# A tower block of attention and mixture of experts: one half of each weighing goes between the next group's two units of scores, the other half behind that group's fill

## The chip, the cores and the metric

One NeuronCore of one Trainium2 chip runs the whole program. The metric is the device time of one execution in microseconds (us), here the median of three runs.

## The reference

The input is x, 4 images of 64 channels and 64 x 64 pixels. Three steps follow one another:

```python
h = tok(x)                    # 1x1 conv, batch norm, relu, 1x1 conv to 9 filters per pixel,
                              # then each pixel is the sum of its 3x3 neighbours times those filters
h = h + attn(layernorm(h))    # 4 images, 4096 rows of 64: softmax(Q K^T / 8) V, one head
h = h + ffn(layernorm(h))     # each row of 64 goes to the best of 32 experts: 64 -> 16 -> 64, relu
```

In attention Q, K and V are the layer norm's rows times a 64 x 64 matrix plus a bias; each of the 4096 rows of an image is weighed against all 4096 rows of it. All is fp32.

## The kernel before, in words

**Blocks and groups.** An image is four blocks of 1024 query rows, so there are 16 blocks n. Each block's attention runs over 16 groups g of 256 key rows. Q K^T is folded into one matrix: `g_t` holds a block's queries times that matrix, `keys_t` the transposed layer norm's rows. A group has two units of scores (`score`, L573), each four matmuls of 64x64 by 64x512 into half of the PSUM tensor `scores`. In the profile an fp32 matmul is two records, so such a unit is eight. Behind each unit ScalarE takes the exponential of 128x1024 scores into a slot of `probs` (L736), a ring of four slots. Weighing (`into_z`, L583) multiplies a group's exponentials with `keys` and adds into `z_ps`, over all 16 groups of a block: eight matmuls, four for each of two tiles r of keys. The two exponentials of a group are both needed for either tile.

**The order on TensorE** is written out by hand, in the loop over n and g at the end of the TensorE program (from L658). In each group stand: the two units of scores of group g, then the fills of the group, then the weighing of group g-1. The weighing of a block's last group, 15, comes in the next block's group 0, behind its two units of scores. VectorE then waits for `pv_done`, adds the two halves of `z_ps` into `z_sb` (L1011, L1013) and raises `z_copied`; the first weighing of the new block waits for that.

**Fills** are the other work of TensorE. A table (`opening_groups` to `whole_plan`, from L79) says which fills stand in which group. Those the text speaks of, for a block m whose attention is done (behind(m), groups of the next block): `pz` in group 3 (z times the value matrix, L521; VectorE drains it from L918 on, and goes on to the residual and the second layer norm), `yt` in 6 (transposes, L448), `lg` in 7 (router logits, L527; drained by VectorE at L928), `fin` in 8 (transposes of block m-1's expert output, L564; it waits until lg is drained, as both use the same PSUM banks), `ot` in 10, `hid0` to `hid3` in 11 to 14 (first expert matrix, L539 and L543; ScalarE drains them at L729) and `o2` in 15 (L556). For blocks to come: `cc` and `cv` (the two small convolutions, L483 and L493; cc or cv stands in group 1 of blocks 1, 2, 4, 6, 8 and 10), `xt` (L448) and `g` (L513), which turn the layer norm's rows into `keys_t` and `g_t`. In block 0, xt stands in groups 3, 7 and 11, g in 4, 8 and 12, and the scores of groups 4, 8 and 12 wait for ScalarE's copy of xt (L721).

**VectorE** works its list in order: z's copy, then `sum0`, `sum1`, `sum2` (the taps of the dynamic convolution of a block four ahead, L856 and L861, in groups 0, 2 and 4 of the plan, then its layer norm), with pz between sum1 and sum2 and lg behind sum2. Blocks 12 to 15 have no sums. In block 0 it works the sums of blocks 1 to 3, whose filters come by DMA.

Of the kernel before, what the change touches and what calls it, by code (L numbers as in the profile page):

```python
# [24 lines left out]
BLOCKS = B * NQ  # L25
PAIRS = TILES // 2
# [133 lines left out]
def vit_block_kernel(nc, x, once, kept, out):  # L160
# [5 lines left out]
    with ExitStack() as ctx:  # L166
# [3 lines left out]
        def sem(name):  # L170
            return ctx.enter_context(nc.semaphore(name))
# [76 lines left out]
        scores_ready, probs_ready, pv_done = sem("scores_ready"), sem("probs_ready"), sem("pv_done")  # L248
        scores_ready_again, probs_ready_again = sem("scores_ready_again"), sem("probs_ready_again")
        pv_done_again = sem("pv_done_again")  # L250
        z_copied = sem("z_copied")
# [14 lines left out]
        def groups_of(n):  # L266

            return [(g, plan[n].get(g, [])) for g in range(-1, PAIRS + 1)]
# [13 lines left out]
        def rows_of(r):  # L282
            return slice(64 * r, 64 * r + 64)
# [136 lines left out]
        def _(pe):  # L420
# [6 lines left out]
            def wait_drained(fill):  # L427
                pe.wait_ge(drained[banks_of.sem[fill]], banks_of.nth[fill])
# [140 lines left out]
            def score(n, g, c):  # L569

                for r in range(2):
                    for h in range(2):
                        last = T.matmul(scores[rows_of(h), c, r * 512:(r + 1) * 512],  # L573
                                        keys_t[rows_of(r), n // NQ % 2, g * 128 + 64 * h:g * 128 + 64 * h + 64],
                                        g_t[rows_of(r), n % GRING, c, :], start=True, stop=True)
                return last

            def into_z(n, g):

                for r in range(2):  # L580
                    for h in range(2):
                        for c in range(2):
                            last = T.matmul(z_ps[rows_of(c), h, :], keys[rows_of(h), n // NQ % 2, 2 * g + r, :],  # L583
                                            probs[rows_of(h), (2 * g + c) % RING, r * 512:(r + 1) * 512],
                                            start=(g == 0 and r == 0), stop=(g == PAIRS - 1 and r == 1))
                return last

            def usual_score(n, g):
                for c in range(2):
                    unit = (n * PAIRS + g) * 2 + c  # L590
                    if unit > 1:
                        pe.wait_ge(probs_ready, unit - 1)
                    score(n, g, c).then_inc(scores_ready, 1)

            def usual_weigh(n, g):
                if g == 0 and n:
                    pe.wait_ge(z_copied, n)
                pe.wait_ge(probs_ready, (n * PAIRS + g) * 2 + 2)
                into_z(n, g).then_inc(pv_done, 1)

            def attend_again():
                into_z(0, PAIRS - 1)
                for g in range(PAIRS):
                    for c in range(2):
                        if g or c:
                            pe.wait_ge(probs_ready_again, max(1, 2 * g + c - 1))
                        score(0, g, c).then_inc(scores_ready_again, 1)
                    if g:
                        pe.wait_ge(probs_ready_again, 2 * g)
                        into_z(0, g - 1).then_inc(pv_done_again, 1)  # L610
                pe.wait_ge(probs_ready_again, 2 * PAIRS)
# [35 lines left out]
            def shift_if_needed(b):  # L647
                pe.wait_ge(flag_ready, 1)
                with pe.If(pe.value_load(flag[0:1, 0:1], min_val=0, max_val=1)):
                    find_max(b)  # L650
                    if b == 0:
                        attend_again()
                with pe.Else():
                    pe.sem_inc(max_scores_ready, 4 * TILES)
                    pe.sem_inc(shifted_ready, S // 512)

            pe.wait_ge(kept_first_loaded, 16)
            for n in range(BLOCKS + 1):  # L658
                b = n // NQ
                if n % NQ == 0 and 0 < b < B:  # L660
                    wait_drained(f"xt@{n + NQ - 1}")
                    wait_drained(f"g@{n + NQ - 1}")
                    shift_if_needed(b)
                for g, names in groups_of(n):
                    if n < BLOCKS and 0 <= g < PAIRS:
                        if n == 0 and g % (PAIRS // NQ) == 0:
                            wait_drained(f"xt@{g // (PAIRS // NQ)}")
                        if g == 0:
                            wait_drained(f"g@{n}")
                        if n == 0 and g == 0:  # L670

                            pe.wait_ge(flag_ready, 1)
                        usual_score(n, g)
                    if g == 0 and n:
                        usual_weigh(n - 1, PAIRS - 1)
                    for full in names:
                        fill(full)
                    if n < BLOCKS and 0 < g < PAIRS:
                        usual_weigh(n, g - 1)
                if n == 0:  # L680
                    shift_if_needed(0)
                    pe.wait_ge(pool_weights_ready, 1)
# [411 lines left out]
```

## Time and profile before

| | us |
|---|---|
| median of 3 runs | 1241.97 (1240.64 to 1242.17) |
| the profiled execution | 1238.29 |
| its span, first to last instruction | 1236.2 |
| TensorE matmul busy | 1156.3 |
| ScalarE busy | 623.8 |
| VectorE busy | 496.5 |
| mean granted TensorE clock | 0.984 |

The profile is one execution, and the rows further down are all from it. Rows of matmuls give the start of the first record, and the time to the modelled end of the last one. Matmuls on different quarters of the array run at the same time.

### The profile page before, as it was taken

The page shows a single profiled execution, that of the slowest core. Times are in us where ns is not written, and L with a number is a line of the kernel's source. Part 1 is how long each engine was busy: PE and PEld are TensorE (multiplying, and loading weights), DVE is VectorE, ACT ScalarE, POOL GpSimd, SP SyncE. Part 2 cuts the span into 40 slices and gives each one's busy share as a digit, 9 for nine tenths or more (in the row PEclk, how much of TensorE's full clock was granted, in tenths as well). Part 3 has the DMA queues.
Part 4 walks back from the last instruction along what each step waited for, and adds up shares of the span by engine and source line. Part 5 has one row for each costly group of instructions (what it writes and reads, how often), then busy time and mean ns, then how long its engine had stood idle before and what let it go on. Part 6 is the DMA issues. An engine that isn't in the chain of part 4 may idle for free.

```text
span 1236.2 us, 28064 instructions
## 1 busy us (share of the span) xinstructions
PE 1156.3 (94%) x12122; PEld 464.9 (38%) x12122; DVE 496.5 (40%) x1130; ACT 623.8 (50%) x664; POOL 10.1 (1%) x36
## 2 busy tenths in 40 slices
PE   7698999999999999999999999999999999999965
PEld 2133434333343433434343333434334333434431
DVE  4882774518072452707245170724403030313131
ACT  1255555555555455555555555554555555554611
POOL 3000000000000000000000000000000000000000
PEclk9999999999999999999999999999999999999986
DMA  5543231201214120121212012121000000000000
GB/s 139 120 114 89 70 89 27 63 2 31 57 28 98 27 61 1 32 58 28 60 28 55 10 34 54 27 62 27 10 2 10 1 2 10 1 10 1 10 1 18
DMA packets 11886, 48.42 MB, mean 39 GB/s; under 512 B 2462, under 2 KB 2590, under 8 KB 11372
## 3 DMA queue, kind: packets, MB, share of 16 engines
q1 hardware_dynamic: 11756, 46.53, 15.8%
q8 instruction: 101, 1.65, 0.6%
q14 instruction: 29, 0.24, 0.1%
HBM read 41.77 MB, written 4.75 MB: 38 GB/s over the span
## 4 chain that ended last, share of the span: by engine, by line
PE 68%; DVE 20%; DVEq 4%; issue 4%; ACT 2%; DMA 2%; SPq 0%; ACTq 0%
PE z_ps L583 26%; PE scores L573 24%; PE both L556 5%; DVEq L803 4%; PE both L543 4%; DVE hres L861 4%; DVE tap_product L856 2%; PE both L448 1%; PE z_ps L473 1%; DVE tap_product L828 1%; DVE tap_product L826 1%; DVE stat L824 1%; DVE stat L830 1%; DMA filter_ring<-filters 1%; ACT hidden L729 1%
## 5 line engine op out<-in xcount | busy, mean ns | idle before, releaser
L736 ACT ACTIVATE probs<-scores 128x1024 f32<-128x1024 f32 x480 | 465.4, 1021 | 472.7 <-PE scores L573 472.7
L573 PE MATMUL scores<-g_t,keys_t 64*64 64x512 f32 x4096 | 506.1, 592 | 3.1 <-issue 2.9
L583 PE MATMUL z_ps<-probs,keys 64*64 64x512 f32 x4096 | 506.6, 593 | 0.2 <-DVE z_sb L1013 0.2
L573 PEld LDWEIGHTS scores<-g_t,keys_t 64*64 64x64 f32 x4096 | 170.3, 134 | 281.8 <-issue 275.7
L583 PEld LDWEIGHTS z_ps<-probs,keys 64*64 64x64 f32 x4096 | 160.7, 133 | 230.3 <-issue 204.6
L946 DVE COPY o_sb<-both 128x512 f32<-128x512 f32 x16 | 11.1, 692 | 487.0 <-PE both L556 487.0
L861 DVE TENSOR_TENSOR hres<-hres,tap_product 128x504 f32<-128x504 f32 (+1 forms) x128 | 88.0, 688 | 10.8 <-issue 0.5
L856 DVE SCALAR_TENSOR_TENSOR tap_product<-filter_ring,w,xin 128x504 f32<-128x504 f32 (+1 forms) x120 | 89.0, 742 | 6.1 <-DMA filter_ring<-filters 2.2
L729 ACT ACTIVATE hidden<-both 128x1024 f32<-128x1024 f32 x64 | 65.5, 1023 | 10.0 <-PE both L543 10.0
L543 PE MATMUL both<-y_t,w 64*64 64x512 f32 x512 | 70.0, 618 | 0.0
L556 PE MATMUL both<-hidden,w 64*64 64x512 f32 x512 | 66.2, 604 | 0.0
L736 ACT ACTIVATE probs<-scores,first_scale 128x1024 f32<-128x1024 f32 x32 | 34.1, 1111 | 22.7 <-PE scores L573 22.5
L1011 DVE COPY z_sb<-z_ps 128x512 f32<-128x512 f32 x16 | 11.1, 692 | 81.9 <-PE z_ps L583 81.9
L556 PEld LDWEIGHTS both<-hidden,w 64*64 64x64 f32 x512 | 27.1, 136 | 25.0 <-issue 23.6
L513 PE MATMUL both<-keys_t,a_w 64*64 64x512 f32 x128 | 18.2, 639 | 14.7 <-ACT hidden L729 12.6
L539 PE MATMUL both<-onehot_t,mask_w 64*64 64x512 bf16 x256 | 26.3, 392 | 4.2 <-ACT hidden L729 3.4
L543 PEld LDWEIGHTS both<-y_t,w 64*64 64x64 f32 x512 | 20.2, 138 | 22.7 <-issue 18.9
L564 PE MATMUL both<-w,o_sb 64*64 64x64 f32 x512 | 11.3, 228 | 15.3 <-DVE logits L928 13.6
L725 ACT COPY g_t<-both 128x1024 f32<-128x1024 f32 x16 | 16.2, 1012 | 16.7 <-PE both L513 16.7
L448 PE MATMUL both<-w,keys 64*64 64x64 f32 x512 | 10.9, 225 | 13.8 <-DVE keys L837 13.8
L828 DVE TENSOR_TENSOR tap_product<-tap_product 128x512 f32<-128x512 f32 x32 | 22.2, 693 | 2.4
L830 DVE TENSOR_REDUCE stat<-tap_product 128x8 f32<-128x512 f32 x32 | 22.0, 686 | 2.3
(113 smaller groups left out, 542.9 us busy)
## 6 DMA issues: line engine op xcount, KB each, us to landing
filter_ring<-filters SPq DMA_DIRECT2D x90, 384.0 KB, 5.4
out_dram<-out_sb SPq DMA_DIRECT2D x32, 128.0 KB, 2.4
xin<-x_dram SPq DMA_DIRECT2D x6, 528.0 KB, 7.4
hidden<-once_dram SPq DMA_DIRECT2D x1, 930.0 KB, 12.8
hidden<-once_dram SPq DMA_DIRECT2D x1, 576.0 KB, 4.5
filters<-filters_sb SPq DMA_DIRECT2D x30, 18.0 KB
xin<-x_dram SPq DMA_DIRECT2D x1, 384.0 KB, 6.2
xin<-x_dram SPq DMA_DIRECT2D x1, 368.0 KB, 7.3
```

The source lines that it names most:

```text
L539: T.matmul(both[rows_of(c), r, :], mask_w[rows_of(r), f * 128 + 64 * c:f * 128 + 64 * c + 64], onehot_t[rows_of(r), :], start=True, stop=F ...
L543: last = T.matmul(both[rows_of(c), r, :], w1[rows_of(r), f * 128 + 64 * c:f * 128 + 64 * c + 64], y_t[rows_of(r), :], start=False, stop=True)
L556: last = T.matmul(both[rows_of(r), h, :], w2[rows_of(h), f, :], hidden[rows_of(h), f, r, :], start=(f == 0 and h != r), stop=(f == FT - 1))
L573: last = T.matmul(scores[rows_of(h), c, r * 512:(r + 1) * 512], keys_t[rows_of(r), n // NQ % 2, g * 128 + 64 * h:g * 128 + 64 * h + 64], g ...
L583: last = T.matmul(z_ps[rows_of(c), h, :], keys[rows_of(h), n // NQ % 2, 2 * g + r, :], probs[rows_of(h), (2 * g + c) % RING, r * 512:(r + ...
L729: A.activation(hidden[:, int(name[3:]), :, :], both[:, :, :], ACT.Relu).then_inc(done, 1)
L736: A.activation(probs[:, unit % RING, :], scores[:, c, :], ACT.Exp, scale=SCALE if n else first_scale[:, 0:1]).then_inc(probs_ready, 1)
L803: dve.drain()
L828: V.tensor_tensor(squares[:, :, :], centred[:, :, :], centred[:, :, :], ALU.mult)
L830: V.reduce_sum(total, squares[:, :, :], AX_X)
L856: product = V.scalar_tensor_tensor(dst, flt, keep["b2c"][:, t:t + 1], pix, ALU.add, ALU.mult)
L861: V.tensor_tensor(mine[:, :, lo:hi], mine[:, :, lo:hi], dst, ALU.add)
```

## The change

`into_z` takes the tiles of keys that it is to weigh. `usual_score` is one unit, `usual_weigh` one tile r of the two; the first tile has the waits (for `z_copied` in group 0, and for both exponentials), the second raises `pv_done`. In a group the order is now: scores unit 0, weighing of the group before with tile 0, scores unit 1, fills, weighing of the group before with tile 1. The other engines' programs are not touched.

```diff
-            def into_z(n, g):
-
-                for r in range(2):
+            def into_z(n, g, tiles=range(2)):
+
+                for r in tiles:
...
-            def usual_score(n, g):
-                for c in range(2):
-                    unit = (n * PAIRS + g) * 2 + c
-                    if unit > 1:
-                        pe.wait_ge(probs_ready, unit - 1)
-                    score(n, g, c).then_inc(scores_ready, 1)
-
-            def usual_weigh(n, g):
-                if g == 0 and n:
-                    pe.wait_ge(z_copied, n)
-                pe.wait_ge(probs_ready, (n * PAIRS + g) * 2 + 2)
-                into_z(n, g).then_inc(pv_done, 1)
+            def usual_score(n, g, c):
+                unit = (n * PAIRS + g) * 2 + c
+                if unit > 1:
+                    pe.wait_ge(probs_ready, unit - 1)
+                score(n, g, c).then_inc(scores_ready, 1)
+
+            def usual_weigh(n, g, r):
+                if r == 0:
+                    if g == 0 and n:
+                        pe.wait_ge(z_copied, n)
+                    pe.wait_ge(probs_ready, (n * PAIRS + g) * 2 + 2)
+                last = into_z(n, g, [r])
+                if r:
+                    last.then_inc(pv_done, 1)
+
+            def behind_by_one(n, g):
+                return (n, g - 1) if g else (n - 1, PAIRS - 1)
...
-                        usual_score(n, g)
-                    if g == 0 and n:
-                        usual_weigh(n - 1, PAIRS - 1)
+
+                        for k in range(2):
+                            usual_score(n, g, k)
+                            if k == 0 and (n or g):
+                                usual_weigh(*behind_by_one(n, g), 0)
+                    elif g == 0:
+                        usual_weigh(*behind_by_one(n, g), 0)
                     for full in names:
                         fill(full)
-                    if n < BLOCKS and 0 < g < PAIRS:
-                        usual_weigh(n, g - 1)
+                    if 0 <= g < PAIRS and (n or g) and (n < BLOCKS or g == 0):
+                        usual_weigh(*behind_by_one(n, g), 1)
```

On TensorE, at the change from block 2 to block 3 (rows in pairs: the first matmul of a unit with its waits, then the others of it). Before, from the last weighing of block 2 to the first of block 3:

```order
L583 MATMUL z_ps<-probs,keys 64x512 [waits probs_ready]
L583 MATMUL z_ps<-probs,keys 64x512 x7
L573 MATMUL scores<-g_t,keys_t 64x512 [waits probs_ready]
L573 MATMUL scores<-g_t,keys_t 64x512 x3
L573 MATMUL scores<-g_t,keys_t 64x512 [waits probs_ready]
L573 MATMUL scores<-g_t,keys_t 64x512 x3
L583 MATMUL z_ps<-probs,keys 64x512 [waits probs_ready,z_copied]
L583 MATMUL z_ps<-probs,keys 64x512 x7
```

Now, from the second half of the last weighing of block 2 to the first unit behind the wait:

```order
L583 MATMUL z_ps<-probs,keys 64x512 x4
L573 MATMUL scores<-g_t,keys_t 64x512 [waits probs_ready]
L573 MATMUL scores<-g_t,keys_t 64x512 x3
L583 MATMUL z_ps<-probs,keys 64x512 [waits probs_ready,z_copied]
L583 MATMUL z_ps<-probs,keys 64x512 x3
L573 MATMUL scores<-g_t,keys_t 64x512 [waits probs_ready]
```

The second unit of scores has moved from before the wait for `z_copied` to behind it.

On TensorE around fin (L564, 16 transposes) in group 8 of block 3, between lg (L527) and the weighing behind fin. Before:

```order
L527 MATMUL both<-router_w,y_t 128x64 x4
L583 MATMUL z_ps<-probs,keys 64x512 x8
L573 MATMUL scores<-g_t,keys_t 64x512 x8
L564 MATMUL both<-w,o_sb 64x64 x16
L583 MATMUL z_ps<-probs,keys 64x512 x8
```

Now:

```order
L527 MATMUL both<-router_w,y_t 128x64 x4
L583 MATMUL z_ps<-probs,keys 64x512 x4
L573 MATMUL scores<-g_t,keys_t 64x512 x4
L583 MATMUL z_ps<-probs,keys 64x512 x4
L573 MATMUL scores<-g_t,keys_t 64x512 x4
L564 MATMUL both<-w,o_sb 64x64 x16
L583 MATMUL z_ps<-probs,keys 64x512 x4
```

Between the two fills stand four units as before, but half of group 7's weighing now stands ahead of fin, where all of it stood behind.

## Rows read from the trace of the kernel before

**Rows 1.** The page: busy time of TensorE, and the chain that ended last by engine

```profile
PE 1156.3 (94%) x12122; PEld 464.9 (38%) x12122; DVE 496.5 (40%) x1130; ACT 623.8 (50%) x664; POOL 10.1 (1%) x36
...
PE 68%; DVE 20%; DVEq 4%; issue 4%; ACT 2%; DMA 2%; SPq 0%; ACTq 0%
```

**Rows 2.** The page's groups: busy us, mean ns of one, idle before

```profile
L736 ACT ACTIVATE probs<-scores 128x1024 f32<-128x1024 f32 x480 | 465.4, 1021 | 472.7 <-PE scores L573 472.7
```

**Rows 3.** Timeline, middle of block 3: start us, us, engine, what

```profile
276.63 1.90 PE L573 MATMUL scores<-g_t,keys_t 64*64 64x512 f32 x16
...
277.74 1.94 ACT L736 ACTIVATE probs<-scores 128x1024 f32<-128x1024 f32 x2 [1.59 <-PE scores L573]
...
278.35 1.90 PE L583 MATMUL z_ps<-probs,keys 64*64 64x512 f32 x16
```

**Rows 4.** Timeline, change from block 2 to block 3

```profile
271.02 2.27 PE L583 MATMUL z_ps<-probs,keys 64*64 64x512 f32 x16
...
272.73 2.27 PE L573 MATMUL scores<-g_t,keys_t 64*64 64x512 f32 x16
...
273.36 0.69 DVE L1011 COPY z_sb<-z_ps 128x512 f32<-128x512 f32 x1 [3.70 <-PE z_ps L583]
...
274.12 0.69 DVE L1013 TENSOR_TENSOR z_sb<-z_sb,z_ps 128x512 f32<-128x512 f32 x1
...
274.87 1.95 PE L583 MATMUL z_ps<-probs,keys 64*64 64x512 f32 x16
```

**Rows 5.** Timeline, change from block 3 to block 4, with a fill (L483)

```profile
345.89 0.69 DVE L1013 TENSOR_TENSOR z_sb<-z_sb,z_ps 128x512 f32<-128x512 f32 x1
...
346.22 1.41 PE L483 MATMUL both<-xin,conv_w 64*64 64x512 f32 x8
...
347.08 2.27 PE L583 MATMUL z_ps<-probs,keys 64*64 64x512 f32 x16
```

**Rows 6.** Timeline, pz and what VectorE starts behind it, blocks 3, 4, 5

```profile
281.89 1.16 PE L521 MATMUL both<-wv_w,z_sb 128*128 128x130 f32 x8
...
283.11 0.17 DVE L918 RECIPROCAL stat<-both 128x4 f32<-128x4 f32 x1
...
354.43 1.16 PE L521 MATMUL both<-wv_w,z_sb 128*128 128x130 f32 x8
...
355.63 0.18 DVE L918 RECIPROCAL stat<-both 128x4 f32<-128x4 f32 x1 [0.66 <-PE both L521]
...
425.84 1.16 PE L521 MATMUL both<-wv_w,z_sb 128*128 128x130 f32 x8
...
427.42 0.18 DVE L918 RECIPROCAL stat<-both 128x4 f32<-128x4 f32 x1
```

**Rows 7.** Timeline, lg drained by VectorE, and fin, block 3

```profile
303.38 0.42 DVE L928 COPY logits<-both 128x256 f32<-128x256 f32 x1
...
303.85 0.69 PE L564 MATMUL both<-w,o_sb 64*64 64x64 f32 x32 [1.81 <-DVE logits L928]
```

**Rows 8.** Waits: engine, line, for whom: us in total, times, longest

```profile
DVE stat L918 <- PE both L521: 38.4, 11, 8.3
...
PE both L564 <- DVE logits L928: 13.6, 11, 1.8
...
PEld z_ps L583 <- DVE z_sb L1013: 7.1, 9, 1.1
```

**Rows 9.** Timeline, the last xt of block 0

```profile
102.79 0.69 PE L448 MATMUL both<-w,keys 64*64 64x64 f32 x32 [3.03 <-DVE keys L837]
...
103.28 1.93 PE L583 MATMUL z_ps<-probs,keys 64*64 64x512 f32 x16
...
103.54 0.59 ACT L721 COPY keys_t<-both 128x512 f32<-128x512 f32 x1 [2.46 <-PE both L448]
```

**Rows 10.** Stretches: us, busy by engine, granted clock (1.00 is full), DMA, GB/s

```profile
269.00:341.00 72.00, 69.05 (x754) 27.41 (x750) 30.86 (x70) 37.54 (x40) 0.00 (x0) 1.00 0.16 38
...
84.00:87.00 3.00, 3.00 (x16) 0.96 (x12) 2.76 (x5) 0.12 (x1) 0.00 (x0) 0.50 0.00 0
```

## The prediction

> **What bounds the kernel now.** I read the page's head and groups first, then the timeline at the places where the order changes, and the waits last. TensorE is busy 1156.3 us, 94% of the span, and carries 68% of the chain that ended last; VectorE carries 20% [rows 1]. ScalarE is no bound: an exponential takes 1021 ns of it for every two units of TensorE [rows 2]. I call four fp32 matmuls of 64x512 a unit (eight records), whether they are one unit of scores or half a weighing. In the middle of a block, pieces of two units start 1.72 us apart (276.63, 278.35), so a unit costs 0.86 us [rows 3]. There nothing is waited for, and regrouping the same units can win nothing by itself. What the change can move is what TensorE waits for at the few places where another engine answers:
> - *z at the change of block.* The last weighing of block 2 ends at 271.02 + 2.27 = 273.29; VectorE adds the two halves until 274.81, and the first weighing of block 3 starts at 274.87, 1.58 after that end [rows 4]. Two units of scores stand between and hide nearly all of it: the ends 273.29 and 276.82 are 3.53 apart where four units need 3.43, so 0.10 is lost. (I compare ends, since matmuls can start in pairs, skewed, with no gain in rate.) Where a fill stands there too, as in block 4, nothing is lost: the ends 347.63 and 349.35 are 1.72 apart [rows 5].
> - *pz in group 3.* Its result goes to VectorE, which is there just then: in block 3 it starts 0.06 after the fill's end (281.89 + 1.16 = 283.05, start 283.11), in block 4 it has waited 0.66, in block 5 it comes 0.42 late [rows 6].
> - *fin in group 8* waits until VectorE has drained lg: 1.81 us in block 3 [rows 7], 13.6 us over 11 times [rows 8]. VectorE is on the path from z through pz to here.
> - *xt in block 0*, which waits for VectorE's layer norm: 3.03 us at the last of them [rows 9].
>
> **The change, part by part.** No instruction's work is added or taken away; 4 matmuls of each weighing move to before the second unit of scores of the next group.
>
> (a) *The wait for z.* The last half of block n-1 now ends after both of block n's first two units of scores, and one unit, not two, stands before the next block's first half, which waits for z. VectorE's part is the same 1.58 us. From the end E of the last half: scores end at E + 0.86, the half starts at E + 1.58 and ends 1.09 later (the row of two units after such a wait is 1.95 long [rows 4], less 0.86) at E + 2.67, where E + 1.72 would be due: 0.95 lost. Behind the wait stand the second unit of scores, then the fill of group 1, which gives no cover any more. Extra at each change of block: 0.95 - 0.10 = 0.85 without a fill there, 0.95 with one. Blocks 1, 2, 4, 6, 8 and 10 have the fill.
>
> (b) *What VectorE then waits for.* From z's release to pz there were 8 units (7.02 us with the restart, 274.87 to 281.89 [rows 4, 6]); now 10, as the halves of scores 1 and weighing 2 shift across. So in block 3 pz ends at 274.87 + 7.02 + 1.72 + 1.16 = 284.77 and VectorE goes on at 284.81 by the 0.04 of block 4: 1.70 later than before. Its run to lg, and with it fin, comes 1.70 later; TensorE arrives at fin 1.72 later, so the wait of 1.81 there stays. The steps between (yt in group 6 behind y, xt behind the layer norm) move with both. In block 4 z is released at 345.89 + 0.69 + 0.06 = 346.64; 10 units and the fill's one give pz at 346.64 + 7.02 + 1.72 + 0.86 = 356.24 for 354.43: 1.81 later, and VectorE the same, since it had been waiting already. In block 5: pz ends at 427.00 + 1.72, VectorE goes on at 428.76 for 427.42: 1.34.
>
> (c) *One unit less behind the fills.* Since a half now goes ahead of each fill, one unit less is left between fin and the next z: -0.86 in each block. Net per block: with a fill 1.81 - 0.86 = 0.95 (six blocks: 5.7); blocks 3, 9, 11 as block 3, 1.70 - 0.86 = 0.84 (2.5); blocks 5, 7 as block 5, 1.34 - 0.86 = 0.48 (1.0). I sort them by the 11 waits at L918 [rows 8]: six of about 0.66 and five of the light blocks leave five blocks that come late. Blocks 12 to 15 have neither fin on the path nor sums: 4 x 0.85 = 3.4.
>
> (d) *Block 0.* Its last xt is set by VectorE and DMA, which the change does not touch, and one unit less is left behind it: -0.86. But the next scores need ScalarE's copy of xt (103.54 + 0.59 = 104.13) and now have one unit of cover, 103.28 + 0.86 = 104.14 [rows 9]: about 0.06 back. Net -0.8.
>
> (e) *The half's wait for exponentials.* It needs the second exponential of the group before. That unit of scores ends at e; by the timeline the exponential starts 0.07 later (the first unit ends at 276.63 + 1.90 - 0.86 = 277.67, the exponential starts at 277.74 [rows 3]), takes 1.02, and 0.06 later the half may start: e + 1.15. It is due at e - 0.18 + 1.72 = e + 1.54. In skewed stretches (rows of 2.27 instead of 1.90) the start is due at e - 0.57 + 1.72 = e + 1.15: no margin, no loss. ScalarE's drains of fills still fit, as a group is as long as before. Costed at nothing; the cover is 0.39 us, and if it went, each group would pay the rest.
>
> (f) *More changes between scores and weighings*, some 500 of them more. [Rows 3] show such a change in step with the rest; to the 0.01 the rows resolve, it could be worth 5 us either way, and I take zero, as the starts there stand 1.72 apart like any two pieces.
>
> Sum: 5.7 + 2.5 + 1.0 + 3.4 - 0.8 = **+11.8 us**. The profiled execution took 1238.29 (span 1236.2) and would take 1250.1; the median of the three runs is 1241.97, 3.7 above it, so I forecast 1253.8.
>
> **A rule that speaks against it more.** The granted clock stood at full, 2.4 GHz, through block 3 with its wait of 1.81 (1.00), and stood at half of it, 1.2 GHz, at 84 to 87 us, behind the opening [rows 10]. The Trainium skill, "TensorE: Matmul & The Clock Gate", section "A second HAM failure mode: psum-queue depth-cycling", says that brief pauses between groups of matmuls can make the clock swing between its levels; by it the sum would have a term of its own for the clock instead of none (its size by rows: case 3 below). The trace disagrees so far: waits at fin as long as the new one, in block after block, did not do it.
>
> **The rivals.**
> 1. *Not slower: fin swallows the delay.* If VectorE were not held at pz, the wait at fin would shrink by up to 1.81 us. The ten blocks 2 to 11 would pay 5 x 0.95 + 5 x 0.85 = 9.0 and get back nearly all of the 13.6 us [rows 8], say 13.3; block 1 and blocks 12 to 15 pay 4.4, block 0 gives 0.8: 9.0 - 13.3 + 4.4 - 0.8 = -0.7, so 1241.3. It decides by where VectorE is when pz is filled: it needs to be 1.7 us late there, and [rows 6] show 0.06 and 0.42 and a wait. Also in this case: a gain from (f). Chance 0.09.
> 2. *Slower still: the halves wait for ScalarE.* If an exponential's answer came 0.05 us too late for each of 240 halves (the margin in skewed stretches is none), 12 us more: 1266. Against it: the unskewed margin of 0.39, and that rows turn unskewed after any wait. Chance 0.08.
> 3. *The clock falls at each z.* The 3 us from 84 to 87 at half clock did 1.5 us of work [rows 10]; one such stretch at each of 15 changes of block is 22 more, 1276. Against it: the full clock beside the wait of 1.81. Chance 0.02.
> 4. *It does not do what it says*: the hardware queue already holds matmuls of the other kind ready, and order makes no difference: 1242. Against it: a wait for z stops whatever is behind it [rows 4]. Chance 0.02.
>
> **How the numbers follow.** Forecast 0.79, on 1253.8. Term (f) reaches 5 us either way, 1249 to 1259; (c) has 1 us of doubt in the sorting of blocks. The range adds a little on both sides for a partial case 1 or 2: 1247 to 1260. A measurement of this kernel tells 0.2% (2.5 us) from nothing. Faster 0.04, same 0.08 (case 1 in the main), slower 0.88.
>
> **What would show it.** In the changed profile the wait at the first half's weighing for z_sb grows from 9 waits of 7.1 us in all [rows 8] to 15, each some 0.85 longer; VectorE's wait at L918 for pz is there in all 16 blocks, about 1.7 us in blocks 3, 5, 7, 9 and 11 (0.4 less in two of them) and some 2.5 in the even ones to 10; the wait at fin stays near 13 us in sum; the granted clock as before. Wrong if fin's wait vanishes (case 1), if matmuls of the weighing sit idle for probs in mid-block (case 2), or if pieces of one unit do not start 0.86 apart.

## The result, and the profile after

The change made the kernel slower: 1254.4 us (median of 4, 1253.3 to 1255.25) against 1241.5 for the kernel before on the same chips; ratio 1.0104, 95% interval 1.0086 to 1.0121, so 12.9 us. The profiled execution took 1255.04 us with a span of 1252.9; that is 16.7 more than the span before and not 12.9, since the execution profiled before (1238.29) was faster than any of its four timed ones, and this one is near the slow end of its own four.

The page of the changed kernel, for [rows 1]: TensorE's matmuls are busy 4.8 us longer, and the rest of the 16.7 us of span is idle time. ScalarE's 27.6 us are no new work: two exponentials in a row took 1.94 us together [rows 3], and most of them now stand apart, at 1.02 each.

```profile
PE 1161.1 (93%) x12122; PEld 455.7 (36%) x12122; DVE 496.7 (40%) x1130; ACT 651.4 (52%) x664; POOL 10.1 (1%) x36
...
PE 72%; DVE 18%; DVEq 3%; issue 3%; ACT 2%; DMA 2%; SPq 0%; ACTq 0%
```

Its timeline at the change from block 2 to block 3, for [rows 4] (the file's lines moved: z's copy is L1020 and L1022 now):

```profile
278.24 1.41 PE L583 MATMUL z_ps<-probs,keys 64*64 64x512 f32 x8
279.10 1.41 PE L573 MATMUL scores<-g_t,keys_t 64*64 64x512 f32 x8
...
279.72 0.69 DVE L1020 COPY z_sb<-z_ps 128x512 f32<-128x512 f32 x1 [2.84 <-PE z_ps L583]
280.49 0.69 DVE L1022 TENSOR_TENSOR z_sb<-z_sb,z_ps 128x512 f32<-128x512 f32 x1
...
281.23 1.09 PE L583 MATMUL z_ps<-probs,keys 64*64 64x512 f32 x8 [0.72 <-DVE z_sb L1022]
282.14 1.04 PE L573 MATMUL scores<-g_t,keys_t 64*64 64x512 f32 x8
```

The last half ends at E = 278.24 + 1.41 = 279.65. One unit of scores follows, the first half of the new block starts at E + 1.58 and ends at E + 2.67: the figures of the sum.

Its waits, for [rows 8]:

```profile
DVE stat L927 <- PE both L521: 63.6, 16, 10.0
...
PEld z_ps L583 <- DVE z_sb L1022: 24.4, 15, 2.0
...
PE both L564 <- DVE logits L937: 12.8, 11, 1.8
```

All 15 changes of block wait for z now, where 9 did; VectorE waits for pz in all 16 blocks; and the wait at fin is nearly as long as it was (13.6 before). The middle row is of TensorE's weight loads, which run ahead of its matmuls: they stand idle for 1.60 us at a change, where it was 0.74 in a block without a fill and nothing in the six with one (at the change into block 13 it is 0.38 more, before and now). The matmuls themselves stand idle for about 0.72 of it. Behind pz, for [rows 6], VectorE starts in blocks 3, 4 and 5 after

```profile
291.17 0.18 DVE L927 RECIPROCAL stat<-both 128x4 f32<-128x4 f32 x1 [1.62 <-PE both L521]
...
364.64 0.18 DVE L927 RECIPROCAL stat<-both 128x4 f32<-128x4 f32 x1 [2.47 <-PE both L521]
...
436.91 0.18 DVE L927 RECIPROCAL stat<-both 128x4 f32<-128x4 f32 x1 [1.25 <-PE both L521]
```

and fin in block 3, for [rows 7], still stands idle for 1.80:

```profile
311.92 0.69 PE L564 MATMUL both<-w,o_sb 64*64 64x64 f32 x32 [1.80 <-DVE logits L937]
```

Where the time came from is best read between the first and the last copy of z, the stretch of blocks 1 to 15. The rows of that instruction, of the kernel before and then of the changed one (shortest, median and longest in ns, then first and last start):

```profile
L1011 DVE COPY z_sb<-z_ps x16: 691/692/693, 128.4 to 1188.4; 128x512 f32<-128x512 f32 x16
```

```profile
L1020 DVE COPY z_sb<-z_ps x16: 690/691/692, 132.0 to 1205.5; 128x512 f32<-128x512 f32 x16
```

1060.0 us became 1073.5 (first start to last start): the 15 blocks cost 13.5 us. The other 3.6 us of this profile lie ahead of the first z, in the opening and block 0.

### The profile page after: what moved, and what is told of

Same layout as the page of the kernel before. It is cut to its first block, busy times and chain, and to the rows that moved or that the text cites. A ratio compares the mean times of both kernels' runs of the same rounds, so it can differ in the third digit from the quotient of the medians.

```text
span 1252.9 us, 28064 instructions
## 1 busy us (share of the span) xinstructions
PE 1161.1 (93%) x12122; PEld 455.7 (36%) x12122; DVE 496.7 (40%) x1130; ACT 651.4 (52%) x664; POOL 10.1 (1%) x36
## 4 chain that ended last, share of the span: by engine, by line
PE 72%; DVE 18%; DVEq 3%; issue 3%; ACT 2%; DMA 2%; SPq 0%; ACTq 0%
PE z_ps L583 27%; PE scores L573 26%; PE both L543 5%; PE both L556 5%; DVEq L812 3%; DVE hres L870 2%; PE both L448 1%; PE both L521 1%; PE z_ps L473 1%; DVE tap_product L837 1%; DVE tap_product L835 1%; DVE stat L839 1%; DVE stat L833 1%; DMA filter_ring<-filters 1%; PE both L539 1%
## 5 line engine op out<-in xcount | busy, mean ns | idle before, releaser
L745 ACT ACTIVATE probs<-scores 128x1024 f32<-128x1024 f32 x480 | 491.2, 1023 | 459.3 <-PE scores L573 459.3
L583 PE MATMUL z_ps<-probs,keys 64*64 64x512 f32 x4096 | 557.4, 594 | 11.4 <-DVE z_sb L1022 10.1
L573 PE MATMUL scores<-g_t,keys_t 64*64 64x512 f32 x4096 | 555.8, 593 | 2.9 <-issue 2.6
L573 PEld LDWEIGHTS scores<-g_t,keys_t 64*64 64x64 f32 x4096 | 166.9, 134 | 285.2 <-issue 260.9
L583 PEld LDWEIGHTS z_ps<-probs,keys 64*64 64x64 f32 x4096 | 157.3, 133 | 251.6 <-issue 203.6
L1020 DVE COPY z_sb<-z_ps 128x512 f32<-128x512 f32 x16 | 11.1, 691 | 72.9 <-PE z_ps L583 72.9
L513 PE MATMUL both<-keys_t,a_w 64*64 64x512 f32 x128 | 18.2, 639 | 14.7 <-ACT hidden L738 12.6
L927 DVE RECIPROCAL stat<-both 128x4 f32<-128x4 f32 x32 | 5.7, 177 | 63.6 <-PE both L521 63.6
L448 PE MATMUL both<-w,keys 64*64 64x64 f32 x512 | 11.2, 228 | 15.1 <-DVE keys L846 14.3
L734 ACT COPY g_t<-both 128x1024 f32<-128x1024 f32 x16 | 16.2, 1010 | 16.7 <-PE both L513 16.7
L564 PE MATMUL both<-w,o_sb 64*64 64x64 f32 x512 | 11.4, 228 | 14.4 <-DVE logits L937 12.8
```

Of the source, the lines that this page charges most:

```text
L448: last = T.matmul(both[rows_of(a), h, j * 64:(j + 1) * 64], tiles[2 * j + a][rows_of(h)], ident[rows_of(h), rows_of(h)], start=True, stop= ...
L745: A.activation(probs[:, unit % RING, :], scores[:, c, :], ACT.Exp, scale=SCALE if n else first_scale[:, 0:1]).then_inc(probs_ready, 1)
```

## The experiments

Each kernel was timed against the kernel before in 5 rounds on one chip (of e9 there is one execution). Two experiments that ran on different chips are compared by their ratios to the kernel before. In e1, e2, e3, e7 and e9 a condition `halved(n, g)` says which weighings are cut, n and g being the block and group in which they are issued; the others stand whole where they stood before.

### e1: the old cover for z, everything else cut

```diff
+            def halved(n, g):
+                return g != 1
```

> The change, but the first weighing of each block (group 0, done in group 1) stays whole behind both units of scores and the fill, as before. Theory (the whole loss hangs on the one wait for z): the cover is back, blocks 2 to 15 cost nothing or save 0.4 (blocks 5 and 7), block 1 keeps 0.9 of loss at its group 16, block 0 saves 0.8: about 1241, ratio 0.998 to 1.001. Rival (480 more changes between scores and weighings, or halves waiting for ScalarE, cost the time): 1250 or more, since nearly all halves are still there. Rival (clock spells in block 0): 1.5 to 2 us above the first figure.

Measured: 1241.39 us, ratio 1.0004 (0.9995 to 1.0013). With 239 of the 255 weighings still cut, the loss is gone. The timeline at the same change of block has the two units together ahead of the wait again (first row, a skewed pair as in [rows 4]), and behind it the cut groups run without a gap, 0.86 us from start to start:

```profile
276.07 2.27 PE L573 MATMUL scores<-g_t,keys_t 64*64 64x512 f32 x16
278.20 1.95 PE L583 MATMUL z_ps<-probs,keys 64*64 64x512 f32 x16
279.97 1.04 PE L573 MATMUL scores<-g_t,keys_t 64*64 64x512 f32 x8
280.82 1.04 PE L583 MATMUL z_ps<-probs,keys 64*64 64x512 f32 x8
281.68 1.04 PE L573 MATMUL scores<-g_t,keys_t 64*64 64x512 f32 x8
```

From one copy of z to the next, each of blocks 2 to 15 takes what it took before to 0.02 us, but for blocks 5 and 7, which are 0.40 and 0.37 shorter, as expected. So neither the cuts nor ScalarE's answers in mid-block cost anything that a measurement can tell: the rival of halves that wait for ScalarE falls.

### e2: only the first weighing of each block cut

```diff
+            def halved(n, g):
+                return g == 1 and n > 0
```

> The kernel before, but with the first weighing of each of blocks 1 to 15 cut in two halves round the second unit of scores; all other weighings whole. Theory: the same loss as the change from 15 places alone: 6 x 0.95 + 3 x 0.85 + 2 x 0.47 + 4 x 0.86 = 12.6 us, 1254, ratio 1.009 to 1.011. Rival (the many halves in mid-block cost it): 1242 to 1243, as only 15 of 255 weighings are cut.

Measured: 1254.43 us, ratio 1.0109 (1.0093 to 1.0124). Fifteen cuts bring the whole loss. The first to the last copy of z is 12.6 us longer than before (1072.6), the expected sum to the tenth:

```profile
L1029 DVE COPY z_sb<-z_ps x16: 690/692/693, 129.5 to 1202.1; 128x512 f32<-128x512 f32 x16
```

### e7: no cover at all

The condition is that of e2; the lines are against e2's kernel.

```diff
+                        if halved(n, g):
+                            usual_weigh(*behind_by_one(n, g), 0)
                         for k in range(2):
                             usual_score(n, g, k)
-                            if k == 0 and (n or g) and halved(n, g):
-                                usual_weigh(*behind_by_one(n, g), 0)
```

> As e2, but the first half of each block's first weighing stands ahead of both units of scores of group 1, so that nothing covers the wait for z. Theory (each unit of cover taken away costs its 0.86 us): 15 x 0.86 = 12.9 us over e2's 1254.4: 1267, ratio 1.021. Rival (the cut itself costs, whatever stands ahead): 1254, as e2.

Measured: 1267.87 us, ratio 1.0215 (1.0198 to 1.0233). By the ratios, one unit of cover less costs 13.5 us (e2) and two units less 26.7: each unit taken from ahead of the wait costs about its own length 15 times. From the first to the last z it is 1087.2 us (133.8 to 1221.0), 14.6 over e2 where 12.9 were expected. Blocks 2 to 15 are 0.85 to 0.89 over e2 each; the rest, 1.7 us, lies in block 1, which begins at a granted clock of 0.78 in this profile (132 to 138 us). At the change into block 3:

```profile
285.57 1.09 PE L583 MATMUL z_ps<-probs,keys 64*64 64x512 f32 x8 [1.58 <-DVE z_sb L1031]
```

Now TensorE is idle for the whole of VectorE's 1.58 us.

### e3: the change in block 0 alone

```diff
+            def halved(n, g):
+                return n == 0
```

> The change in block 0 alone; all later blocks in the order before. Theory: one unit less behind the last xt saves 0.8 us, 1240.7, unless stretches at half clock come behind the longer wait for that xt: then up to 3 us more, 1244. The profile tells which by the granted clock from 100 to 132 us. Rival (halves cost by themselves): 0.05 us or more at each of 15 weighings, seen as starts further apart than 0.86 us per unit.

Measured: 1240.05 us (median of 11) against 1241.15, ratio 0.9993 (0.9984 to 1.0002): the right size, but no change is inside the interval. TensorE comes earlier to the last xt, waits longer there, and is at half clock right behind it; stretches of e3 (us, busy by engine, granted clock, DMA, GB/s):

```profile
103.00:108.00 5.00, 4.95 (x60) 2.31 (x64) 0.00 (x0) 1.53 (x2) 0.00 (x0) 0.68 0.80 172
124.00:132.00 8.00, 7.06 (x60) 3.30 (x64) 1.97 (x3) 3.49 (x4) 0.00 (x0) 1.00 0.02 4
```

### e4 and e5: fin out of VectorE's way, without and with the change

```diff
-    return {3: at(m, "pz"), 6: at(m, "yt"), 7: at(m, "lg"), 8: at(m - 1, "fin"), 10: at(m, "ot"),
+    return {3: at(m, "pz"), 2: at(m - 1, "fin"), 6: at(m, "yt"), 7: at(m, "lg"), 10: at(m, "ot"),
...
-    return merged(ahead, {0: at(i, "sum0"), 2: at(i, "sum1"), 4: at(i, "sum2")}, behind(n - 1),
+    return merged(ahead, behind(n - 1), {0: at(i, "sum0"), 2: at(i, "sum1"), 4: at(i, "sum2")},
```

> The kernel before with fin in group 2 instead of group 8 (VectorE drains it ahead of sum1). Theory (VectorE holds TensorE at fin in blocks 2 to 11, because fin's banks wait for lg): 13.6 us of idle and some 0.1 to 0.4 a time go, VectorE has 4 us of slack for its list until xt and ot: 1227 to 1229, ratio 0.989. Rival (VectorE's list bounds the block anyway, and the wait moves to xt in group 9 or ot in group 10): 1238 or more.

> The change with fin in group 2, as in e4. Theory: with no wait at fin, every change of block pays its full 0.86 (no fill) or 0.95 (fill), and the savings of blocks 5 and 7 are gone: 6 x 0.95 + 9 x 0.86 + 0.9 (block 1, group 16) - 0.8 (block 0) = 13.5 us over e4's 1226.7: 1240, ratio 0.999 to the kernel before. Rival (without the hold at fin the delay behind z is swallowed elsewhere): 1227 to 1232.

Measured: e4 1226.67 us, ratio 0.9887 (0.9872 to 0.9902); e5 1241.23 us, ratio 1.0003 (0.9994 to 1.0012). The wait at fin was a real hold. Without it the change costs 14.4 us by the two ratios; that this is more than the 12.9 with it is inside their intervals, and is told by the rows of z. From first to last z, e5 takes 1059.0 us (130.6 to 1189.6) and e4 1044.6 (130.7 to 1175.3): 14.4, where the expected terms without block 0 give 14.3, and where it was 13.5 with the hold. Blocks 5 and 7 pay 0.85 each here.

### e6 and e8: g behind o2 instead of behind hid1

```diff
-                  {9: at(i, "xt"), 12: at(i, "g")})
+                  {9: at(i, "xt"), 16: at(i, "g")})
```

in e6, and in e8 `12 if i % NQ == NQ - 1 else 16`; both on top of e4.

> The kernel before with fin in group 2 and, in blocks 2 to 11, g in group 16 instead of behind hid1 in group 12. Theory: 10 waits of 1.3 us for ScalarE's drain of hid1 go; at the changes into blocks 4, 8 and 12 the first scores now wait some 1.1 us for g's drain: 13 - 3.3 = about 10 us under e4's 1226.7: 1217, ratio 0.981. Rival (g then waits for VectorE's drain of o2 in group 16, or the drain of g delays the exponentials of group 0): 1222 or more.

> As e6, but in blocks 3, 7 and 11, behind which a new image begins, g stays in group 12. Theory (in e6 the wait for g's drain stands ahead of the branch on the flag, so that the branch is reached with nothing queued, 2.9 us a time): blocks 3, 7 and 11 take 69.7 us as in e4 instead of 71.4: 5 us under e6, 1217.4, ratio 0.981. Rival (the loss lies with g in group 16 of any block): 1222 or more.

Measured: e6 1222.35 us, ratio 0.9856 (0.9835 to 0.9876), by the ratios a gain of 4 over e4 where 10 was expected. Its timeline at the change to the second image shows what was missed:

```profile
337.54 1.09 PE L513 MATMUL both<-keys_t,a_w 64*64 64x512 f32 x8
338.69 1.01 ACT L725 COPY g_t<-both 128x1024 f32<-128x1024 f32 x1 [5.45 <-PE both L513]
341.33 1.95 PE L573 MATMUL scores<-g_t,keys_t 64*64 64x512 f32 x16 [2.70 <-issue]
```

The wait for g's drain stands ahead of the branch on the flag that opens each image. Of the 2.70 us of idle time 1.07 are the wait for the drain, which ends at 339.70; the expectation had that. The scores start only 1.63 after it. In the kernel before, the weighing of group 14 is the last work ahead of the branch, g had long been drained, and no idle time shows there; here TensorE has nothing left to do when the wait ends. From z to z, each of blocks 3, 7 and 11 takes 1.62 to 1.66 more than in e4, and each of the other seven with g moved 1.3 less: 4.0 in all. Whether the load of the flag, the branch or what follows it takes the 1.63 was not separated. e8 keeps g where it was in the three blocks before a new image: 1217.16 us (median of 5), ratio 0.9799 (0.9783 to 0.9815), as expected; blocks 3, 7 and 11 are back at e4's 69.7 us. The waits of e8 at g:

```profile
PE both L513 <- ACT hidden L729: 4.6, 4, 1.1
```

12.6 us over 11 times have become 4.6 over 4, and no wait at fin for lg is left. e8 beats the kernel before by 2.0% and the changed one by 3.0%.

### e9: block 1

```diff
-                return g != 1
+                return g != 1 and (n, g) != (1, 15)
```

> As e1, and in block 1 the weighing of group 14 stays whole behind o2. Theory (in group 16 of block 1, xt waits for VectorE's drain of o2, and half a weighing covers 0.86 us less of it than a whole one): from the z of block 0 to the z of block 1 TensorE takes 0.86 us less than in e1, as in the kernel before. Rival: as in e1.

Measured: 1242.52 us in its one execution. In e1 the second copy of z starts at 204.16, 73.27 behind the first (130.89); in e9 205.71 is 72.4 behind the first (133.3); in the kernel before it was 72.42 (128.39 to 200.81). The expected 0.86 is there (0.85 to 0.87), in one profile. This row, here of the changed kernel, is without its wait in e9:

```profile
200.17 0.69 PE L448 MATMUL both<-w,keys 64*64 64x64 f32 x32 [0.72 <-DVE o_sb L957]
```

## Why the prediction was right, point by point

- **The sum.** +11.8 was forecast, 12.9 measured; 1253.8 and 1254.4 us. Block by block, from the start of z's copy of the block before to that of its own (us, some of the 15):

| block | 1 | 2 | 3 | 4 | 5 | 12 |
|---|---|---|---|---|---|---|
| before | 72.42 | 72.55 | 71.77 | 72.17 | 71.80 | 67.04 |
| changed | 74.27 | 73.48 | 72.62 | 73.12 | 72.26 | 67.89 |
| more | 1.85 | 0.93 | 0.85 | 0.95 | 0.46 | 0.85 |
| forecast | 0.95 | 0.95 | 0.84 | 0.95 | 0.48 | 0.85 |
| e1 | 73.27 | 72.53 | 71.76 | 72.17 | 71.40 | 67.03 |
| e2 | 73.41 | 73.47 | 72.60 | 73.12 | 72.25 | 67.89 |
| e7 | 75.97 | 74.33 | 73.49 | 73.98 | 73.13 | 68.75 |

  The blocks that are left out are within 0.02 us of their forecast too (0.95 for 6, 8 and 10, 0.84 for 9 and 11, 0.48 for 7, 0.85 for 13 to 15). Only block 1 is off.
- **(a), the wait for z,** is the cause and of the size worked out. e1 puts only this cover back and the loss goes; e2 takes only this cover away and the loss comes; e7 doubles what is taken and the loss doubles. Only the figure named for its sign was too small: 7.1 and 15 times 0.85 are 19.9 us of waits, and 24.4 were measured, because in the six blocks with a fill the weight loads had not waited at all and now wait the whole 1.60.
- **(b), VectorE held at pz.** It moved as computed: counted from z's copy, VectorE starts behind pz 1.70, 1.80 and 1.33 us later in blocks 3, 4 and 5, for 1.70, 1.81 and 1.34. Its waits there are 1.62, 2.47 and 1.25.
- **(c), one unit less behind fin.** The wait there stayed (12.8 for 13.6). In e5, without the hold at fin, blocks 5 and 7 pay 0.85 and 0.85 for 0.46 and 0.49, as they must if the hold had given the rest back there.
- **The term that was missed** is in block 1. Its group 16 has xt and g behind o2, and xt waits for VectorE's drain of o2. I counted what stands ahead of each fill, but (b) and (c) only for fins and pz: between o2 and this xt stood a whole weighing, and now a half. That cost 0.9, by which block 1 is off in the table; e9, whose group 15 has the whole weighing back behind o2, is without it, and so is e2, where block 1 has it too (73.41 for the 74.27 of the changed kernel). With it the blocks' 12.6 become 13.5, which is what the two rows of z's copy give.
- **(d), block 0.** -0.8 was forecast. e3 gives -1.1 us in the median, with nothing inside its interval. The profile of the changed kernel itself shows 3.6 us more ahead of the first z. Part is the opening (TensorE's first wait for x is 5.8 us for 5.3), most is the clock. Its stretches are these; by an estimate, length times the missing share of the clock, they lack 1.7 and 3.4 us, against 1.5 in the one stretch of the kernel before:

```profile
103.00:108.00 5.00, 4.65 (x56) 2.20 (x60) 0.21 (x1) 1.08 (x2) 0.00 (x0) 0.66 0.73 164
124.00:132.00 8.00, 7.41 (x38) 3.05 (x40) 0.03 (x1) 2.04 (x2) 0.00 (x0) 0.57 0.01 2
```

  The kernel before had 1.00 in both, but a stretch at half clock at 84 to 87 [rows 10]. Five experiments have the old block 0, and all of them have a fall at 103 to 108 too: 0.73 in e2, 0.66 in e4 and e8, 0.50 in e6 and e7; at 124 to 132, e8 has 0.79 and e7 0.62. So such stretches come and go in block 0 in either order, and one profile is no measure of it. The first copy of z starts at 128.4 (before), 129.5, 130.7, 131.2, 133.8 and 130.8 (e2, e4, e6, e7, e8) with the old block 0, and at 132.0 (changed), 130.9, 129.8, 130.6 and 133.3 (e1, e3, e5, e9) with the new one. Whether the change makes them more frequent stays open; e3's median says that it is no large effect.
- **(e) and (f)** were costed at nothing, and e1 shows nothing: 0.02 us at most in a block with 15 cuts. In the changed kernel no matmul of the weighing stands idle for an exponential in mid-block.
- **The rivals.** Not slower, because fin swallows the delay: wrong by [rows 6], as VectorE was itself on TensorE's clock at pz, and fin's wait did not shrink. Halves that wait for ScalarE: excluded by e1. A fall of the clock at each z: the granted clock is full through the blocks of the changed kernel (1.00 from 132 to 1204 us), and in e7, with waits twice as long, from 200 to 1221 us. Order makes no difference: excluded by e2.

## What to carry to other kernels

Before a piece of work is moved ahead, look for what stands between each wait and the signal it waits for: here four matmuls of cover, moved at one of 16 places in a block, cost 12.6 of the blocks' 13.5 us, one place in block 1 cost the other 0.9, and the rest of the moves cost nothing. Where every unit is needed anyway, regrouping wins only at places where another engine's answer is late; the gain was at those places (fin behind lg, g behind hid1), by moving the fill, not the weighing. Nor was a wait that two engines pass to each other cover here: the idle 1.8 us at fin could not take up a delay, because the engine it waited for had been delayed by the same work.

## What the runs showed that I had not expected

At the branch that opens an image TensorE shows no idle time in the kernel before, with a weighing as the last work ahead of it (blocks 4, 8 and 12), and in e6 it is idle for 1.63 us behind a wait that stands right before it. But work ahead of the branch is not all: at the same branch behind block 0 a weighing stands ahead as well (it ends at 120.66), and yet the kernel before is idle there, as are the other runs (2.07 to 2.56 us):

```profile
122.86 1.93 PE L573 MATMUL scores<-g_t,keys_t 64*64 64x512 f32 x12 [2.20 <-issue]
```

One more wait stands behind the branch there; no experiment tells what makes the difference. And half-clock stretches in block 0 come at different places from run to run of the same instruction order (before, e2, e4, e6, e7, e8 in their block 0), where the first z starts anywhere from 128.4 to 133.8 us: the differences of under 0.2% here could only be read block by block, where the rows of blocks 2 to 15 agree to 0.03 us between runs of the same order.
